# Additions on GpSimd held behind two norms, and three steps placed elsewhere ahead of the second scan

## What is computed

```python
x = x + _layernorm(_L0_attn_ref(_layernorm(x), ...))   # state-space scan, 16 states
x = x + _layernorm(_L0_ffn_ref(_layernorm(x), ...))    # the "sign layer"
x = x + _layernorm(_L1_attn_ref(_layernorm(x), ...))   # second scan, 16 states
x = x + _layernorm(_L1_ffn_ref(_layernorm(x), ...))    # 16 experts, top 2, and a shared one

# sign layer: out = einsum(sign(xn * gamma + beta), sign(weight - mean(weight))) + bias) * alpha
# scan: h = exp(delta * A) * h + delta * B * x ;  y = sum over states of h * C, plus x * D
# with delta = softplus(x @ W_delta @ W_dt + b_dt), B = x @ W_B, C = x @ W_C
```

## Time and profile before

| what | value |
| --- | --- |
| three runs | 686.29, 688.40, 689.64 us; median 688.4 us |
| the profiled execution | 688.48 us, its span (first to last instruction) 686.7 us |
| mean granted TensorE clock | 0.975 of full speed |
| busy share of the span | PE 91%, DVE 77%, ACT 73%, POOL 61% |
| chain that ended last, by engine | PE 64%, DVE 15%, ACT 8%, POOL 8%, issue 3%, DMA 1% |
| stretch between the scans (206 to 291 us) | DVE 74.6 of 85 us busy, ACT 60.3, PE 59.2, POOL 25.7 |
| second scan (291 to 446 us) | PE 153.6 of 155 us busy, ACT 150.3, DVE 147.9, POOL 147.5 |

### The profile page before, as it was taken

One profiled execution on the slowest core, in us unless ns is written; L12 is line 12 of the kernel. 1 busy time (PEld: TensorE's weight loads), 2 busy tenths in 40 slices (PEclk: granted clock), 3 DMA queues, 4 the chain that ended last, 5 costly groups with the idle time before them and its releaser, 6 DMA issues.

```text
span 686.7 us, 12401 instructions
## 1 busy us (share of the span) xinstructions
PE 623.1 (91%) x4334; PEld 533.4 (78%) x4337; DVE 528.3 (77%) x900; ACT 503.8 (73%) x1164; POOL 419.1 (61%) x256
## 2 busy tenths in 40 slices
PE   4779999999992778899999999989999999999994
PEld 2369999999992533799999999977677677777673
DVE  6698999999998899799899999967822644444346
ACT  2999999999974866999999999794544562222244
POOL 0037999999999003189999999980774233333400
PEclk9989999999997799999999999999999999999998
DMA  6022454545450000135445544471232233333183
GB/s 192 4 80 89 161 149 146 149 143 155 138 144 0 1 2 5 70 118 156 154 146 154 147 156 144 127 225 42 78 108 100 77 108 106 101 107 107 63 259 123
DMA packets 57575, 77.83 MB, mean 113 GB/s; under 512 B 8112, under 2 KB 38480, under 8 KB 57520
## 3 DMA queue, kind: packets, MB, share of 16 engines
q1 hardware_dynamic: 53728, 66.75, 32.1%
q0 software_dynamic: 3792, 10.36, 4.2%
HBM read 58.21 MB, written 18.87 MB: 112 GB/s over the span
## 4 chain that ended last, share of the span: by engine, by line
PE 64%; DVE 15%; ACT 8%; POOL 8%; issue 3%; DMA 1%; DVEq 0%; ACTq 0%; POOLq 0%
PE both L1311 16%; PE both L1391 12%; PE bank L1340 12%; POOL arena L1118 7%; PE both L1313 5%; PE bank L1399 3%; PE bank L1400 3%; DVE st L411 2%; DVE arena L645 2%; PE bank L1332 2%; PE bank L1493 1%; DVE residual L572 1%; DVE tok_a L497 1%; PE bank L1452 1%; PE bank L1454 1%
## 5 line engine op out<-in xcount | busy, mean ns | idle before, releaser
L1118 POOL TENSOR_TENSOR arena<-arena,rings 128x1024 f32<-128x1024 f32 x126 | 296.6, 2378 | 17.9 <-DVE arena L645 14.0
L1311 PE MATMUL both<-rings,tok_a 128*128 128x128 f32 x1280 | 182.4, 276 | 3.2 <-DVE arena L645 2.8
L1311 PEld LDWEIGHTS both<-rings,tok_a 128*128 128x128 f32 x1280 | 163.8, 192 | 4.7 <-issue 3.5
L645 DVE TENSOR_TENSOR_SCAN arena<-rings,both 128x1024 f32<-128x1024 f32 x64 | 145.3, 2279 | 13.0 <-PE both L1313 7.8
L645 DVE TENSOR_TENSOR_SCAN arena<-late,both 128x1024 f32<-128x1024 f32 x62 | 140.7, 2278 | 6.7 <-PE both L1313 1.5
L1340 PE MATMUL bank<-ident,arena 128*128 128x128 f32 x1024 | 133.0, 273 | 2.8 <-POOL arena L1118 1.4
L1340 PEld LDWEIGHTS bank<-ident,arena 128*128 128x128 f32 x1024 | 115.7, 141 | 4.2 <-POOL arena L1118 1.9
L1003 ACT ACTIVATE rings<-ident,b_tok 128x128 f32<-128x128 f32 x320 | 106.4, 393 | 0.3
L1159 POOL DMA_INDIRECT y_tok<-rings,dest x47 | 45.1, 959 | 84.9 <-DVE rings L798 84.6
L1003 ACT ACTIVATE rings<-tok_a,b_tok 128x256 f32<-128x256 f32 x192 | 89.5, 499 | 0.0
L1313 PE MATMUL both<-ident,rings 128*128 128x128 f32 x384 | 83.9, 273 | 0.0
(11 more groups left out here) (230 smaller groups left out, 976.3 us busy)
## 6 DMA issues: line engine op xcount, KB each, us to landing
rings<-c_rows SPq DMA_DIRECT2D x128, 256.0 KB, 3.4
w_sb<-w SPq DMA_DIRECT2D x18, 352.0 KB, 4.2
x_sorted<-zeros SPq DMA_DIRECT2D x47, 128.0 KB, 3.4
rings<-x_sorted SPq DMA_DIRECT2D x47, 128.0 KB, 2.0
arena<-w SPq DMA_DIRECT2D x2, 2048.0 KB, 12.9
residual<-x SPq DMA_DIRECT2D x4, 512.0 KB, 5.9
tok_a<-y_tok SPq DMA_DIRECT2D x4, 512.0 KB, 7.2
w_sb<-y_tok SPq DMA_DIRECT2D x4, 512.0 KB, 8.0
```

The source lines that it names most:

```text
L645: dve.tensor_tensor_scan(h_s, decay_s.rearrange("p h t -> p (h t)"), both[s % B_RING][:, :], 0.0, ALU.mult, ALU.add).then_inc(h_ready, 1)
L1118: pool.tensor_tensor(h_both, h_both, c_row, ALU.mult).then_inc(hc_ready, 1)
L1311: pe.matmul(o, tok_a[:, c, h * P:(h + 1) * P], v_ring[:, s % V_RING, j, 0:P], start=True, stop=True)
```

## The change

Five edits, all between the two scans:

1. In `vector_middle`, `f_norm` 1 comes ahead of `f_stat` 2.
2. In `pool_middle`'s step `y_add` 2 of this stretch, POOL first waits until DVE has written all eight chunks of `f_norm` 0 and 1.
3. `keep` runs at the start of `relu` 0 in place of `err` 2.
4. In `vector_middle`, `b_cols` 1 comes ahead of `err` 3.
5. In `scalar_middle`, `decays` is cut in two: the first pair behind `proj` 3, the second between `u_turn` 0 and `log` 3. `bc` 3 comes ahead of `log` 2, and `exp` 3 ahead of `u_turn` 0.

```diff
         vector_middle = [
-            ("y_stat", 2), ("y_stat", 3), ("y_add", 2), ("f_stat", 0), ("f_stat", 1), ("y_add", 3), ("f_norm", 0), ("f_stat", 2),
-            ("f_norm", 1), ("f_norm", 2), ("f_stat", 3), ("r_stat", 0), ("r_add", 0), ("f_norm", 3), ("x_stat", 0), ("r_stat", 1),
+            ("y_stat", 2), ("y_stat", 3), ("y_add", 2), ("f_stat", 0), ("f_stat", 1), ("y_add", 3), ("f_norm", 0), ("f_norm", 1),
+            ("f_stat", 2), ("f_norm", 2), ("f_stat", 3), ("r_stat", 0), ("r_add", 0), ("f_norm", 3), ("x_stat", 0), ("r_stat", 1),
...
-            ("relu", 2), ("dt", 1), ("err", 2), ("relu", 3), ("dt", 2), ("err", 3), ("b_cols", 1), ("dt", 3)]
+            ("relu", 2), ("dt", 1), ("err", 2), ("relu", 3), ("dt", 2), ("b_cols", 1), ("err", 3), ("dt", 3)]
...
-            ("pre", 2), ("exp", 2), ("proj", 3), ("log", 2), ("bc", 3), ("pre", 3), ("u_turn", 0), ("exp", 3), ("decays", 1),
-            ("log", 3), ("u_turn", 1), ("u_turn", 2), ("u_turn", 3)]
+            ("pre", 2), ("exp", 2), ("proj", 3), ("decays", 0), ("bc", 3), ("log", 2), ("pre", 3), ("exp", 3), ("u_turn", 0),
+            ("decays", 1), ("log", 3), ("u_turn", 1), ("u_turn", 2), ("u_turn", 3)]
...
                     if k == 0:
                         ffn_weights()
-                    elif k == Q + 2:
-                        keep()
...
                 elif name == "relu":
+                    if k == Q:
+                        keep()
...
                 elif name == "decays":
-                    for s in range(0, ABAR_RING, 2):
-                        decays(l, s)
+                    decays(l, 2 * q)
...
                 if name == "y_add":
+                    if l == 1 and q == 2:
+                        pool.wait_ge(g_first, 2 * CQ)
                     for c in range(q * CQ, (q + 1) * CQ):
```

## The result

| | kernel before | changed kernel |
| --- | --- | --- |
| median | 688.98 us (12 runs, 685.56 to 696.37) | 683.4 us (12 runs, 683.25 to 685.43) |
| profiled execution, its span | 688.48, 686.7 us | 683.35, 681.4 us |
| mean granted TensorE clock | 0.975 | 0.979 |

The ratio of the comparable runs is 0.9935 (95% interval 0.9919 to 0.9952). Against the median of 688.4 on which the prediction stood this is 5.0 us less; 5.6 were forecast, and 683.4 lies inside its own range.

The account below looks back on a forecast made before the run. Bound: waits between the scans, DVE's first `f_norm` held by POOL, then idle ACT and PE ahead of the second scan. 2.9 + 2.7 = 5.6 us gave 682.8 us; own range 681.0 to 684.6, 8-in-10 range 680.8 to 686.0.

Parts of the forecast that it names:

- The block: DVE's first `f_norm`: one 4559 ns instruction held by POOL's unbroken additions; POOL's wait frees 4.16 us, `f_mm` 0 2.86 earlier.
- The price on ACT: Root of the late `f_stat` 2 stands ahead of `f_mm` 0 in ACT's list: 1.30 of 4.16 us given back.
- Rival 2: Between the scans: POOL's later sums hold `f_stat` 2 and `f_mm` 0 longer, up to 1.3 bound; 684.4 us; chance 0.12.
- I take it as blocked until 226.1: DVE's shift of `f_norm` 2 (L430) waits until POOL's additions end, about 1.4 us; `r_stat` 0 2.8 earlier.
- PE's `f_back` 0 follows `f_mm` 0 by the same 2.9: PE behind the first norms: `f_back` 0 comes 2.9 us earlier, as `f_mm` 0 does.
- The first part: POOL's additions put behind both first norms: the whole stretch from `r_stat` 0 slides 2.9 us earlier; bounds 1.3 and 4.2.
- keep: DVE: its four small instructions fit into 0.88 us idle at `relu` 0; gain at `err` 2 0.57 us.
- ACT's order: Ahead of the second scan: decays and `bc` 3 fill ACT's idle time; `log` 2 0.4, `pre` 3 0.88 us earlier.
- b_cols: DVE ahead of `err` 3: waits 0.5 us for PE's turns, covered by POOL's product; `u_turn` 1's copies 1.8 us earlier.
- Rival 4: `b_cols` holds `err` 3 when PE's turns run at low clock, up to 6.4 us later; 690.1 us; chance 0.05.
- The scan's entry: PE ahead of the second scan: 1.8 us earlier with clock low, 3.0 with it kept up; 2.7 taken.
- rival 1: PE's clock low at the second scan's entry, so only 1.8 us gained there; 683.7 us; chance 0.16.

Follow-up runs that it names:

- e3: The changed kernel without POOL's wait, `f_norm` 1 still ahead of `f_stat` 2; median 684.70 us, ratio to the kernel before 0.9962.
- e10: The changed kernel with ACT's `f_mm` 0 ahead of `f_stat` 2; median 692.27 us (4 runs), ratio to the kernel before 0.9916.
- a_again: The changed kernel once more, same code; median 683.46 us (12 runs), ratio to the kernel before 0.9952, its profiled execution 685.43 us.
- e1: The kernel before with POOL's wait and the exchange of `f_norm` 1 and `f_stat` 2 alone; median 686.26 us, ratio 0.9987.
- e7: The changed kernel with ACT's order of before (decays together, `bc` 3 behind `log` 2, `u_turn` 0 ahead of `exp` 3); 686.54 us.
- e6: The changed kernel with `b_cols` 1 behind `err` 3 on DVE again; 683.22 us.
- e2: The kernel before with the three later moves alone (`keep`, ACT's order, `b_cols` 1); median 685.65 us, ratio 0.9981.
- e12: e10 with `bc` 2 ahead of `log` 1 on ACT and 14 more spare turns behind `u_turn` 1; two runs, medians 693.58 and 681.58 us.
- e8b: The kernel before with one 16-element tensor_scalar more ahead of `f_norm` 0; POOL's first addition to second scan's first step 80.21 us (before 80.01).
- e8: The kernel before with a small two-input instruction and a 16-element tensor_scalar ahead of `f_norm` 0; POOL's first addition to second scan 78.83 us (before 80.01).
- e9: The kernel before with `f_norm` 0 in two-input form; POOL's first addition to second scan's first step 80.17 us (before 80.01).

## Why the prediction was right

**The block.** Right in cause: L554 has no long instruction, POOL's ninth addition came 4.00 us behind the end of its eighth (4.0 by the prediction's times; its list of signs says 3), and e3 shows that it is the wait that does it. From POOL's first addition, `f_mm` 0 moved from 16.15 to 13.36 us: 2.79 earlier against 2.86.

**The price on ACT.** Right: e10 shows that without it `r_add` 0 comes 0.31 earlier, not 1.3, since the statistics of batch 2 are late by then on DVE as well. Rival 2, which had this price grow, got nothing. Its bound of 1.3 was a slip: 1.30 given back twice leaves 4.16 - 2.60 = 1.56.

**What DVE does meanwhile.** The failed step is "I take it as blocked until 226.1". L430 took 0.63 us, not 1.4. `r_stat` 0 thus started without idle time, 3.54 us earlier where 2.8 stood. It needed PE too, and there "PE's `f_back` 0 follows `f_mm` 0 by the same 2.9" was off. Before, then in the changed kernel:

```profile
227.86 1.92 PE L1268 MATMUL both<-ident,tok_a 128*128 128x128 f32 x8
229.57 1.91 PE L1293 MATMUL both<-ident,feat_a 128*128 128x128 f32 x8
```

```profile
224.66 1.92 PE L1269 MATMUL both<-ident,tok_a 128*128 128x128 f32 x8
226.96 1.10 PE L1294 MATMUL both<-ident,feat_a 128*128 128x128 f32 x8 [0.39 <-ACT feat_a L905]
```

Before, `f_back` 0 stood on PE directly behind `f_turn` 1 (L1268) and not behind ACT's `f_mm` 0. `f_turn` 1 came the full 4.16 us earlier, so `f_back` 0, now held by `f_mm` 0 alone, came 3.57 earlier. Had L430 waited for the end of POOL's run, 0.66 us later, `r_stat` 0 would have been 2.9 earlier, as forecast. The clock of PE, 0.92 over 226 to 229 us where it had been 0.50, added nothing that shows: in a_again it was 0.77 and `f_back` 0 took 1.76 us in place of 1.10, and `r_add` 0 came 18.72 us behind POOL's first addition against 18.70. The first part came to 3.40 at `relu` 0, 3.37 in e1, in place of 2.9. This term was under-sized by 0.5.

**`keep`.** Right: four instructions of 0.17 us in DVE's idle time, which went from 0.88 to 0.30, and the pair L512 at `err` 2 took 1.83 us, against the same product. Forecast 0.57; measured 0.57, for L516 behind this pair came 3.97 us earlier and `relu` 0 3.40.

**ACT's order.** Right: `log` 2 without idle time, `pre` 3 4.46 earlier in all, `log` 3 2.0 more than the first part. e7 prices it at 1.5 us by ACT's own work.

**`b_cols`.** The wait was forecast at 0.5 and was 0.62 us, covered as forecast; e6 shows that the move brings nothing. Rival 4 got nothing: PE's turns kept their distance, 64.92 us behind POOL's first addition against 279.48 - 211.16 = 68.32 before, 3.40 earlier, exactly as everything else.

**The scan's entry.** 2.7 was taken between 1.8 and 3.0; the profile shows 2.87 (6.27 less 3.40), with the clock up, so PE's end of the bounds was the right one. In the changed kernel too PE ran turns alone over 277 to 280 us, at 1.00:

```profile
277.00:280.00 3.00, 3.00 (x34) 2.93 (x34) 2.38 (x7) 2.04 (x2) 1.65 (x1) 1.00 0.00 0
```

But rival 1, at 0.16, was wrongly put as an alternative: it happens in some executions of the same kernel. a_again shows it at 1.0 us, inside the 0.9 to 1.2 that the prediction gave.

**The sum.** 3.4 + 2.87 = 6.27 for 5.6. The median moved by less than the gap, 5.0 to 5.6 us by which median of before one takes (688.4 of three runs or 688.98 of twelve). Nine of the changed kernel's twelve executions lie within 683.25 to 683.62, three within 684.54 to 685.43; the low clock at the scan's entry can be part of these, but only a_again's own profile shows it, and there the stretch behind the second scan was longer too, by 1.64 us. What lies outside the gap (a start 0.96 us later in the profiled execution) makes up the rest of that execution. So the total was met within 0.6 us, and partly by luck: an under-sized first part and a remainder that nobody had in the sum offset each other.

## What to carry to other kernels

When one instruction of a group lasts ten times its median and ends with a run on another engine, order the two engines with a wait rather than look for a cheaper form: here a wait of 4 us on POOL bought 3.4 us. Price the wait by what is queued behind it on every engine, and look for the second arrival, which caps both gain and price. Where spare turns hold the clock, count the idle time they leave in the fast case too, since a gain upstream makes it longer. And look at the clock on the way before comparing single profiles: a fall some 38 us ahead, with the same code, decided how much idle time the spare turns left.

## What the runs showed of the hardware

- A held-up DVE instruction can wait over six ends of POOL additions (4.44 to 4.70 us), with sixteen values per partition as with 256. A two-input instruction of four values got in within 0.35 and 0.63 us, and those right behind it one per addition (some 0.77 us each).
- Behind the same idle time of 2.27 to 2.29 us ahead of `proj` 0, its eight products took 3.79 us in nine profiles and 5.44 in five; the changed kernel is in both groups.
- Idle times of PE before `u_turn` 2 of 1.11 to 1.16 us left the clock at 1.00 in four executions (after, e2, both of e12). Behind 2.47 us (e7), 3.05 to 3.06 us (before, e1, e8b) and 4.60 us (e8, e9) it fell. Behind 2.66 or 2.67 us it fell in a_again and e10 and stayed up in e3 and e6: at that length it depends on the execution; in a_again the fall cost 1.0 us.
